# A graph attention layer with pair-routed experts on one core: contexts added in pairs of double width, and the last blocks' leftover work dealt to later slots

## The reference, cut to what matters

```python
x = x + gnn(layernorm(x), adj)   # 4 heads of 32
#   scores = clip(q @ k.T / sqrt(32), -10, 10); where(adj == 0, -10)
#   attn   = softmax over each chunk of 128 keys (8 chunks), ctx = sum over chunks of attn @ v
#   out    = layernorm(ctx @ Wo.T + bo + layernorm(x)) * gamma + beta
x = x + ffn(layernorm(x))        # 8 experts of 128 -> 256 -> 128, exact gelu
#   idx = top_k(x @ Wg + bg, 2); out = sum of the two chosen experts' outputs
```

## Time and profile before

| | |
|---|---|
| median of 3 runs | 776.33 us |
| the profiled execution | 776.3 us, its span 774.2 us |
| busy share of the span | PE 90%, DVE 80%, POOL 75%, ACT 64% |
| granted TensorE clock, mean | 0.973 |
| attention, steps 0 to 127 | to about 546 us |
| slots 0 to 26, with the leftover work | 546.3 to 638.4 us |
| slots 27 to 92, tiles alone | 638.4 us to the last store at 765.1 us |

### The profile page before, as it was taken

The page is one execution under the profiler, slowest core; times in us unless marked ns, Lnnn a source line. Parts: engine busy times, 40 slices in busy tenths (PEclk is TensorE's granted clock), DMA queues, the critical chain, the costliest instruction groups (busy, mean ns, idle before and its releaser), DMA issues.

```text
span 774.2 us, 17066 instructions
## 1 busy us (share of the span) xinstructions
PE 698.8 (90%) x5416; PEld 363.3 (47%) x5416; DVE 623.0 (80%) x1455; ACT 495.4 (64%) x898; POOL 580.1 (75%) x689
## 2 busy tenths in 40 slices
PE   4897999999999999999999999886968869999994
PEld 2222233333333333333333333231668769999994
DVE  4699999999999999999999999899784535545552
ACT  3665567777677776777767776553766426666662
POOL 7569495989879898798987988958477445667664
PEclk9999999999999999999999999997999979999998
DMA  7530000011010110101100001040323223333330
GB/s 264 191 93 28 1 29 14 21 35 47 23 44 21 35 47 23 43 21 36 44 26 29 21 23 42 15 138 29 94 61 92 77 80 88 94 86 99 97 92 1
DMA packets 47959, 45.42 MB, mean 59 GB/s; under 512 B 6982, under 2 KB 42577, under 8 KB 47873
## 3 DMA queue, kind: packets, MB, share of 16 engines
q1 hardware_dynamic: 41888, 31.60, 14.5%
q0 software_dynamic: 5984, 12.74, 4.5%
HBM read 27.73 MB, written 18.34 MB: 60 GB/s over the span
## 4 chain that ended last, share of the span: by engine, by line
PE 43%; DVE 28%; issue 17%; POOL 6%; DMA 2%; ACT 2%; DVEq 1%; POOLq 0%; ACTq 0%
DVE e L940 12%; PE scores_ps L436 11%; PE ctx_ps L448 8%; PE z_ps L455 7%; PE scores_ps L600 5%; POOL out L1412 5%; DVE ctx_part L948 4%; PE ctx_ps L626 3%; PE z_ps L626 3%; DMA near<-in_x 2%; DVE ln_stats L906 2%; PE job_ps L490 2%; PE job_ps L485 2%; DVE best_at L996 1%; DVE z_part L953 1%
## 5 line engine op out<-in xcount | busy, mean ns | idle before, releaser
L739 ACT ACTIVATE e<-e 128x2048 f32<-128x2048 f32 x128 | 244.4, 1910 | 141.5 <-DVE e L940 134.3
L940 DVE SCALAR_TENSOR_TENSOR e<-scores_ps,bound_mem 128x2048 f32<-128x2048 f32 x128 | 292.2, 2283 | 24.6 <-PE scores_ps L436 22.9
L824 ACT ACTIVATE e<-scores_ps,bound_mem 128x128 f32<-128x128 f32 x364 | 104.0, 372 | 67.5 <-PE scores_ps L600 65.0
L1412 POOL DMA_INDIRECT out<-e,near x91 | 91.0, 1000 | 69.1 <-POOL near L1405 27.0
L455 PE MATMUL z_ps<-e,one_column 128*32 128x512 f32 x1024 | 135.5, 601 | 0.0
L1385 POOL TENSOR_TENSOR ctx_part<-ctx_part,z_inv 128x1024 f32<-128x1024 f32 x60 | 114.9, 1914 | 24.7 <-DVE z_inv L956 23.8
L1397 POOL TENSOR_TENSOR ctx_sum<-ctx_sum,ctx_part 128x512 f32<-128x512 f32 x90 | 115.7, 1286 | 6.0
L600 PE MATMUL scores_ps<-e,bound_mem 128*128 128x128 f32 x728 | 100.2, 282 | 2.5 <-DVE bound_mem L1117 1.0
L600 PEld LDWEIGHTS scores_ps<-e,bound_mem 128*128 128x128 f32 x728 | 91.5, 197 | 5.0 <-issue 4.1
L948 DVE STREAM_TRANSPOSE ctx_part<-ctx_ps 128x512 f32<-128x512 f32 x128 | 90.3, 706 | 1.4 <-PE ctx_ps L448 1.3
L1359 POOL DMA_INDIRECT sorted_rows<-x_rows,slot x64 | 63.4, 991 | 18.6 <-issue 17.3
(11 more groups left out here) (171 smaller groups left out, 1031.0 us busy)
## 6 DMA issues: line engine op xcount, KB each, us to landing
near<-sorted_rows SPq DMA_DIRECT2D x91, 130.0 KB
near<-in_x SPq DMA_DIRECT2D x16, 256.0 KB, 2.8
bound_mem<-in_adjT SPq DMA_DIRECT2D x4, 1024.0 KB, 10.5
x_post<-in_x SPq DMA_DIRECT2D x16, 256.0 KB, 2.8
sorted_rows<-pad_row SPq DMA_DIRECT2D x1, 3640.0 KB, 14.9
out<-e,near POOLq DMA_INDIRECT x91
sorted_rows<-x_rows,slot POOLq DMA_INDIRECT x64
bound_mem<-in_w SPq DMA_DIRECT2D x1, 1024.0 KB, 6.6
```

What stands on the lines that cost most here:

```text
L739: nc.scalar.activation(every, every, ACT.Exp, scale=SCORE_SCALE).then_inc(exp_done, 1)
L824: nc.scalar.activation(e_flat[:, h_at:h_at + P], scores_ps[:, i % 2, k * P:(k + 1) * P], ACT.Gelu, bias=part_flat[:, bias_at:bias_at + 1]) ...
L940: dve.scalar_tensor_tensor(out=e[:, s % E_RING], in0=scores_ps[:], scalar=-CLIP, in1=to, op0=ALU.max, op1=ALU.min).then_inc(clipped, 1)
L1412: nc.gpsimd.indirect_dma_start(out=out_rows, out_offset=bass.IndirectOffsetOnAxis(ap=near_u[:, id_at:id_at + 1], axis=0), in_=e_flat[:, at ...
```

## The change

**Contexts in pairs.** POOL's `add_context` becomes `add_pair`: the scaled pair j-2, j-1 is added onto the pair j, j+1 in one 128 x 1024 instruction, in place in `ctx_part`, three times; `add_halves` then adds the two halves of the last pair into `ctx_sum` (128 x 512). DVE does the same for block 15 (`add_last_pair`, `add_last_halves`). Seven adds become four. The semaphore `ctx_added` counts four a block, and the waits of `turn` and `turn_sum` are rewritten for that.

**Leftover work in other slots.**

| what | slot before | slot after |
|---|---|---|
| DVE `scale_last` 0, 2, 4, 6 | 3, 4, 5, 6 | 4, 5, 6, 8 |
| DVE adds of block 15, `turn_sum(15)` | 4 to 6, 7 | 5, 6, 8, 9; 9 |
| POOL `root` of norm 2, ACT normalise, block 14 | 4, 6 | 3, 5 |
| POOL second half of `scatter(13)` | 5 | 8, behind the root of norm 3 |
| PE `project(15)`, DVE statistics 2, block 15 | 8, 8 | 12, 13 |
| PE `turn_xn2(14)`, `gate(14)`, `rank(14)` | 10, 10, 12 | 11, 11, 13 |
| POOL root 2, ACT normalise, POOL residual, block 15 | 8, 10, 10 | 13, 15, 15 |
| DVE statistics 3, POOL root 3, ACT normalise, block 15 | 12, 12, 14 | 16, 16, 19 |
| POOL `scatter(14)` in two halves | 14, 17 | 17, 18 |
| table part 1: `columns`, `ends`, `lookup`, `write_table` | 16, 17, 19, 19 | 16, 18, 21, 21 |
| PE `turn_xn2(15)`, `gate(15)`, `rank(15)` | 19, 20, 22 | 20, 21, 23 |
| POOL `scatter(15)` in two halves | 22, 23 | 24, 25 |
| table part 2: `columns`, `ends`, `lookup`, `write_table` | 23, 24, 25, 25 | 24, 26, 29, 29 |

`pick` is cut in two: `find_owners` (slots 18 and 26) and `find_rows` (19 and 27). `rank(14)` uses the other of the two PSUM banks.

```diff
             def turn(s):
                 dve.wait_ge(ctx_ready, s + 1)
                 u, j = divmod(s - PARTS, CHUNKS)
                 if u >= 0:
-                    need(dve, ctx_added, (CHUNKS - 1) * u + max(j, 1))
+                    need(dve, ctx_added, CHUNKS // 2 * u + j // 2 + 1)
...
+            def add_pair(v, j):
+                to, frm = ctx_pair(v, j), ctx_pair(v, j - 2)
                 pool.wait_ge(ctx_scaled, CHUNKS // 2 * v + j // 2 + 1)
+                need(pool, ctx_added, CHUNKS // 2 * v + j // 2 - 1 if j > 2 else 0)
+                nc.gpsimd.tensor_tensor(to, to, frm, ALU.add).then_inc(ctx_added, 1)
+
+            def add_halves(v):
+                pair = ctx_pair(v, CHUNKS - 2)
+                need(pool, ctxT_ready, v - 1)
+                pool.wait_ge(ctx_added, CHUNKS // 2 * (v + 1) - 1)
+                nc.gpsimd.tensor_tensor(ctx_sum[:, v % 2], pair[:, 0], pair[:, 1], ALU.add).then_inc(ctx_added, 1)
...
-                if k == 8:
-                    project(15)
-                if k == 10:
+                if k == 11:
                     turn_xn2(14)
                 if k == 12:
+                    project(15)
+                if k == 13:
                     rank(14)
                 if k == 16:
                     columns(1)
-                if k == 17:
+                if k == 18:
                     ends(1)
```

More of the change, by code:

```diff
@@ L228, in graph_transformer_layer, with ctx_pair @@
         job_ps = [bank(f"job_ps{k}", [P, BLOCK]) for k in range(2)]
+        def ctx_pair(v, j):
+            at = (CHUNKS * v + j) % PARTS
+            return ctx_part[:, at:at + 2]
         def turned_x2_ps(v):
@@ L959, in scale_last @@
             def scale_last(j):
-                at = (CHUNKS * (BLOCKS - 1) + j) % PARTS
-                pair = ctx_part[:, at:at + 2]
+                pair = ctx_pair(BLOCKS - 1, j)
                 dve.wait_ge(z_inverted, BLOCKS)
@@ L965, in scale_last, with add_last_pair, add_last_halves @@
                                   ALU.mult).then_inc(last_scaled, 1)
-            def add_last(j):
+            def add_last_pair(j):
                 v = BLOCKS - 1
-                to, at = ctx_sum[:, v % 2], (CHUNKS * v + j) % PARTS
+                to, frm = ctx_pair(v, j), ctx_pair(v, j - 2)
                 dve.wait_ge(last_scaled, j // 2 + 1)
[L971 to L977, removed]
+                need(dve, ctx_added, CHUNKS // 2 * v + j // 2 - 1 if j > 2 else 0)
+                dve.tensor_tensor(to, to, frm, ALU.add).then_inc(ctx_added, 1)
+            def add_last_halves():
+                v = BLOCKS - 1
+                pair = ctx_pair(v, CHUNKS - 2)
+                need(dve, ctxT_ready, v - 1)
+                dve.wait_ge(ctx_added, CHUNKS // 2 * (v + 1) - 1)
+                dve.tensor_tensor(ctx_sum[:, v % 2], pair[:, 0], pair[:, 1], ALU.add).then_inc(ctx_added, 1)
             def turn_sum(v):
-                dve.wait_ge(ctx_added, (CHUNKS - 1) * (v + 1))
+                dve.wait_ge(ctx_added, CHUNKS // 2 * (v + 1))
                 need(dve, proj_filled, v)
@@ L1062, in pick, with find_rows @@
                     .then_inc(owner_ready, 1)
+            def find_rows(g):
+                one, n = slice(g, g + 1), GROUPS[g][2] - GROUPS[g][1]
                 dve.wait_ge(owner_ready, g + 1)
@@ L1188, in _ @@
                         if j == 4:
-                            pick(0)
+                            find_owners(0)
+                            find_rows(0)
                         if j == 5:
@@ L1248, in _ @@
                     count_tiles(1)
+                if k == 16:
+                    dve.wait_ge(x2_ready, 16)
+                    statistics(ln["3"], 15, x_rows[:, 15 % 3, :, D:2 * D])
                 if k == 18:
-                    pick(1)
+                    find_owners(1)
                 if k == 19:
+                    find_rows(1)
+                if k == 21:
                     write_table(1)
-                if k == 20:
                     choose(15)
-                if k == 22:
+                if k == 23:
                     place(15)
                     count_rows(2)
-                if k == 23:
+                if k == 24:
                     count_tiles(2)
-                if k == 24:
-                    pick(2)
-                if k == 25:
+                if k == 26:
+                    find_owners(2)
+                if k == 27:
+                    find_rows(2)
+                if k == 29:
                     write_table(2)
@@ L1475, in _ @@
                     scatter(13, (0, 1))
+                if k == 3:
+                    root(ln["2"], 14)
                 if k == 4:
-                    root(ln["2"], 14)
                     add_residual(14)
-                if k == 5:
+                if k == 8:
                     scatter(13, (2, 3))
```

109 lines of the change are left out of this document (46 added, 63 removed).

## The result

The changed kernel takes 785.53 us (median of 6 runs, 782.72 to 787.45) beside 776.74 us of the kernel before (6 runs, 773.45 to 779.43). The ratio is 1.0119, 95% interval 1.0094 to 1.0144: 1.2% slower and clear of noise, where 760 us and "faster" were forecast. The profiled execution took 785.4 us, its span is 783.7 us, 9.5 us more than before.

A forecast was written before the change was run, and what follows sets the result against it. PE's 22.5 us of waits and slow clock between attention's end and slot 27 were the target: -22.5 + 1.5 + 1.5 + 0.7 + 4.0 - 1.3 = -16.1 us, from 776.3 to 760 us, range 753 to 771.

The forecast's parts named there:

- This costs or gives nothing in attention: Pair adds on POOL in attention: saving 2.0 to 0 us a block leaves attention's time unchanged, as POOL has waits there.
- the last block's -1.3: Last attention block: one add fewer lets POOL's scale and residual start earlier, gaining 1.3 us (0 to 2).
- the 0.02 that was left for none of these: Chance 0.02 that neither the forecast nor any of the three rivals comes true.
- POOL's own slack of 23.8 us: Attention: POOL waits 23.8 us in all for the inverted sums, taken as cover for the pair adds.
- A, -5.9: Slot 8: PE's wait for block 15's transposed context ahead of the projection, and the slow clock after, go whole: -5.9 us.
- B, 1.5 of 1.7 kept: Slot 10: of PE's 1.7 us waits for block 14's normalised rows and drained transpose, 1.5 us stays (0 to 3).
- D and E, -5.8 and -9.1: Slots 17 to 18 and 24 to 26: PE's waits at `count_tiles(1)` and `pick(2)`, with slow clock, go: -5.8 and -9.1 us.
- second rival: Slots 17 to 18 and 24 to 26: standstills make the waits, so the new order does not matter there; 768 us, chance 0.12.
- Standstills, +4: DVE and ACT standing idle beside late scatters: costs 6 us if they come back, 0 if not; 4 us taken.
- slower rival: Standstills grow with block 14's and 15's adjacent scatters, PE losing 21.4 us; 779 us, chance 0.05.
- Block 15's chain, +1.5: Slots 15 and 16: block 15's later residual and third statistics delay DVE's copy for tile 17, costing 1.5 us (0 to 4).
- 0.7: Slots: `turn_xn2(15)` one slot after its normalising costs 0.5 us, and small gaps 0.2.

The follow-up runs named there:

- slots kernel with POOL waits: New slots and single adds, plus POOL waiting for DVE's table work in the last attention block; 0.9979 of the kernel before.

## Why the prediction was wrong

**"This costs or gives nothing in attention", and the last block's -1.3.** This step failed, and decides the sign; no rival of mine had it, and 785.5 us lies above the slowest of them (779), in the 0.02 that was left for none of these. I argued from POOL's own slack of 23.8 us and from buffers. The cost was on DVE. Pairs put POOL's wide instructions in other places: the pair add next behind the scatter, 0.4 us after `t_col` starts, and scale and multiply behind it. I had the evidence in the earlier trace rows, and used it for the gain of an earlier scale, not for what would stand there instead. The scale did come earlier, 11.96 us after the block's reciprocal instead of 13.54, and gained nothing. Measured: +6.0 us in the last attention block, +1.8 in block 1, 2 to 3.4 in longer blocks on chip 776; pairs alone 1.0110 and 1.0152. The Trainium skill (SBUF — State Buffer, section "SBUF: two separate sides"), which I used for slots 16 and 17 alone, says that a VectorE instruction with two SBUF inputs and a GpSimd instruction that reads SBUF lock each other out, and that the one that starts first has the ports for the whole instruction. Both held instructions have two SBUF inputs, so the rule names the danger. Its order and length do not come out here: `t_col` starts 0.43 us before the pair add by the trace, was held all the same, and through three wide instructions and not one.

**A, -5.9: right.** There is no wait ahead of the projection in slot 12, and the slow clock there is gone. DVE's pair adds took 1.21 and 1.22 us, as I had taken, its scales 1.23 to 1.29 but for one of 2.10 beside block 14's residual.

**B, 1.5 of 1.7 kept: mis-sized.** I had this chain 0.2 us over. Measured 2.59 us and 2.07 us for a product that takes 1.15: 3.5 us. POOL's root of block 14 stood behind the residual and three stores. With ACT's normalising one slot later the wait was 0.8 us at most.

**D and E, -5.8 and -9.1: the order held, the gain did not.** `ends` and the lookups no longer wait. But most of these waits were made by the standstills or what goes with them: with the old slots on chip 763, `ends(1)` waits for nothing and the lookup of group 2 for 1.55 us instead of 4.66. This was my second rival's mechanism. I gave it 768 us and 0.12. On a chip 776 the runs do not tell the two further apart.

**Standstills, +4: too low.** They came back at both places, and ACT's share with them: PE lost 1.91 and 3.00 us in direct waits, and ran at the lower level after both. By the windows of the two chips they cost up to 14 us in the new order and 10 or 11 in the old. My slower rival had them grow with scatters to 21; its direction was right, its reason (adjacency) is not shown.

**Block 15's chain, +1.5:** 1.74 us of wait and 1.85 instead of 1.13 us for the product behind it, and the next product at 1.92 instead of 1.06 us, 3.4 us in all: inside my 0 to 4, and nearer to the 3.9 us that the prediction worked out for copies held by POOL than to 1.5.

The sum of slots was forecast at -22.5 + 1.5 + 1.5 + 0.7 + 4.0 = -14.8 us and came out at -1.7; on chip 763, without standstills, it is -5.3. Attention was forecast at -1.3 and came out at +11.4; 1.3 us of that was there at the first reciprocal (62.16 instead of 60.82 us), before anything that the change touches, and in the pair of profiles on one chip it was -0.5.

## What to carry to other kernels

Merging or moving an off-path engine's instructions can spend another engine's time: before making GpSimd's elementwise work wider or denser, list every VectorE instruction with two SBUF inputs that may fall beside it, however small, and who waits for it. A wait of GpSimd's for that instruction, ahead of its wide one, protects it and costs GpSimd next to nothing; the place where GpSimd starts again then needs the same look. Where a trace shows idle time of unknown cause, price the change with and without it, and do not book waits behind it as waits of the order.

## What the runs showed of the hardware

- A DVE instruction with two SBUF inputs can be held through more than one GpSimd instruction: 28 elements took 6.01 us through three wide ones, 0.15 us without.
- The hold begins before GpSimd's arithmetic starts by its record (0.43 and 0.69 us before, during an indirect DMA), and not when that arithmetic stands behind a wait, though it starts at the same moment. An indirect DMA alone, with another behind it, held nothing (`owner`, 0.23 us).
- A GpSimd add of two full 128x1024 fp32 inputs takes 2.40 us, the multiply with a broadcast second input 1.92, an add of 128x512 1.29.
- Chips differ: 763.3 us on one and 776.1 to 776.8 on all others for the same kernel. On the slower ones DVE and ACT stood 2 to 6 us beside late scatters, mostly with no engine of the trace as the releaser, and PE was torn too: a lookup's six products, 0.29 us on the other chip, lay over 3.1 us in the slots kernel with POOL waits, with two gaps of 1.2 us and "issue" as their cause. On the faster one none did. The cause is open.
